# Splitting rows into pieces on GpSimd inside the dense stage, and block numbers read 16 at a time, in a three-layer graph network

## What is computed

```python
def _spmm(row, col, vals, x):
    msg = vals[:, None] * x[col]
    return jax.ops.segment_sum(msg, row, num_segments=N)

def _layer(x_prev, row, col, vals, W_a, b_a, W_b, b_b):
    h = _spmm(row, col, vals, x_prev)
    z = (h + x_prev) @ W_a.T + b_a + h * x_prev @ W_b.T + b_b
    return jnp.where(z >= 0, z, NEG_SLOPE * z)

x1 = _layer(x, row, col, vals, W1_1, b1_1, W1_2, b1_2)
x2 = _layer(x1, row, col, vals, W2_1, b2_1, W2_2, b2_2)
x3 = _layer(x2, row, col, vals, W3_1, b3_1, W3_2, b3_2)
return jnp.concatenate((x, x1, x2, x3), axis=1)
```

## Time and profile before

| | us |
|---|---|
| median of 3 runs | 8891.55 |
| the profiled execution | 8889.35 |
| its span, first to last instruction | 8887.5 |
| expand stages, three together | 2430.5 |
| dense stage, each | 78.7 |
| last row of `xb` written to first matmul of the next layer | 33.7 |

### The profile page before, as it was taken

One profiled execution on the slowest core, in us unless ns is written; L12 is line 12 of the kernel. 1 busy time (PEld: TensorE's weight loads), 2 busy tenths in 40 slices (PEclk: granted clock), 3 DMA queues, 4 the chain that ended last, 5 costly groups with the idle time before them and its releaser, 6 DMA issues.

```text
span 8887.5 us, 265258 instructions
## 1 busy us (share of the span) xinstructions
PE 7889.6 (89%) x82756; PEld 7229.6 (81%) x82757; DVE 7142.9 (80%) x9830; ACT 4541.7 (51%) x14097; POOL 5736.8 (65%) x4886
## 2 busy tenths in 40 slices
PE   5999995799996688899999788899999788899999
PEld 4777775577774588789999788899999688799999
DVE  8999988799997877777777777777777777777777
ACT  0999990799995366621112566611112566611112
POOL 4787874588883244478886344478885444488884
PEclk8999995899997799999999899999999899999999
DMA  2111111211111488788887588888886688888885
GB/s 79 7 7 7 7 7 39 34 7 7 7 7 26 159 295 294 289 286 283 286 286 244 204 296 295 302 277 286 286 286 220 228 295 290 296 283 286 286 286 199
DMA packets 877540, 1680.36 MB, mean 189 GB/s; under 512 B 262122, under 2 KB 313399, under 8 KB 876404
## 3 DMA queue, kind: packets, MB, share of 16 engines
q0 software_dynamic: 364832, 907.43, 34.4%
q1 hardware_dynamic: 499692, 758.75, 24.0%
q10 hardware_dynamic: 12520, 6.40, 0.2%
HBM read 912.31 MB, written 759.79 MB: 188 GB/s over the span
## 4 chain that ended last, share of the span: by engine, by line
PE 45%; ACT 19%; issue 12%; DMA 8%; SPq 7%; DVE 5%; POOL 1%; ACTq 1%; DVEq 0%; POOLq 0%
PE ps L1037 35%; ACT hT L723 17%; DMA messages<-work 7%; SPq L684 6%; PE ps L1028 5%; PE ps L864 1%; DVE hT L1348 1%; SPq L669 1%; DVE hT L1134 1%; PE ps L1065 1%; PE ps L1045 1%; PE ps L1066 1%; PE ps L891 1%; POOL work L575 1%; DVE work L1385 1%
## 5 line engine op out<-in xcount | busy, mean ns | idle before, releaser
L1037 PE MATMUL ps<-work 128*128 128x125 f32 x26880 | 3111.5, 278 | 52.6 <-DVE work L1414 52.6
L1037 PEld LDWEIGHTS ps<-work 128*128 128x128 f32 x26880 | 3066.2, 192 | 97.9 <-DVE work L1414 57.4
L603 POOL DMA_INDIRECT work<-messages,work x1680 | 2567.6, 1528 | 557.7 <-issue 550.0
L1028 PE MATMUL ps<-xb,work 125*128 x10752 | 1992.4, 226 | 450.9 <-DVE work L1385 265.8
L792 ACT ACTIVATE work<-ps,work 128x128 f32<-128x128 f32 x5376 | 1526.9, 371 | 1073.4 <-PE ps L1028 572.0
L1414 DVE TENSOR_TENSOR work<-work,iota_p 128x1000 f32<-128x1000 f32 x1680 | 2005.2, 1194 | 1.0 <-ACT work L810 0.4
L1028 PE MATMUL ps<-hT,work 125*128 x10752 | 1991.7, 224 | 0.4
L1028 PE MATMUL ps<-work 125*128 x10752 | 1976.6, 224 | 0.8
L810 ACT ACTIVATE work<-work 128x8 f32<-128x8 f32 x1680 | 516.2, 307 | 2527.8 <-DMA work<-messages,work 2527.8
L917 PEld LDWEIGHTS ps<-hT 128*128 128x128 f32 x12768 | 1484.1, 196 | 297.1 <-ACT stage L712 227.9
L917 PE MATMUL ps<-hT 128*128 128x96 f32 x12768 | 1520.1, 280 | 186.6 <-ACT stage L712 186.5
(11 more groups left out here) (212 smaller groups left out, 6096.0 us busy)
## 6 DMA issues: line engine op xcount, KB each, us to landing
messages<-work SPq DMA_DIRECT2D x2688, 258.0 KB, 4.0
work<-messages,work POOLq DMA_INDIRECT x1680, 5.9
out_x<-xb SPq DMA_DIRECT2D x150, 125.0 KB
sorted_edges<-stage,run_idx POOLq DMA_INDIRECT x798
work<-slot_cols SPq DMA_DIRECT2D x672, 4.0 KB
work<-lane_places SPq DMA_DIRECT2D x532, 5.2 KB, 2.1
out_x<-xb ACTq DMA_DIRECT2D x4, 1562.5 KB
sorted_edges<-hT SPq DMA_DIRECT2D x4, 908.0 KB
```

The costliest lines, as they stand in the source:

```text
L603: pool.indirect_dma_start(out=ck[:, n, :, :].rearrange("p j e -> p (j e)"), out_offset=None, in_=messages, in_offset=bass.IndirectOffsetOn ...
L1028: last = t.matmul(ps[:, n % PR, j * D:(j + 1) * D], col_hot[:, at:at + P], piece[:, bass.ds(offset, D)], start=k == 0, stop=k == 2)
L1037: last = t.matmul(part[n], ck[:, n, j, 0:D], sel[:, n % SELB, j, :], start=j == 0, stop=j == CHB - 1)
```

## The change

First, the split of the rows for the second and third layer. VectorE now splits only the input rows, once, ahead of the layer loop. In the dense stage of every layer, the last too, GpSimd runs 50 steps: it waits until ScalarE has written the two blocks of the step into `xb` and VectorE has read the columns of `hT` that are to be written over (three sums ahead), makes `rest` for 256 columns (125 x 256), waits for that instruction, and makes `x_low` for them. TensorE waits for the last step (`pieces_cut`) where it waited for VectorE's pieces.

Second, TensorE's block numbers. The table is read as bytes: one load takes 16 bytes into 16 registers and serves 16 groups, so the loop has 56 passes a layer instead of 14 and a quarter of the code, and the shift and mask are gone.

```diff
+                def cut_pieces(i, last):
+                    for k in range(DU):
+                        at = bass.ds(i * (DU * 2 * D) + k * 2 * D, 2 * D)
+                        pool.wait_ge(sum_ready, la * DSTEPS + i * DU + (min(k + 3, DU) if last else k + 3))
+                        pool.wait_ge(xb_ready, la * DSTEPS + i * DU + (k + 2))
+                        taken_up()
+                        g.tensor_tensor(rest[:, at], x_flat[:, at], x_high[:, at], ALU.subtract).then_inc(rest_cut, 1)
+                        pool.wait_ge(rest_cut, la * DSTEPS + i * DU + (k + 1))
+                        taken_up()
+                        g.tensor_tensor(x_low[:, at], rest[:, at], x_mid[:, at], ALU.subtract).then_inc(pieces_cut, 1)
+                with pool.Fori(0, DSTEPS // DU - 1) as i:
+                    cut_pieces(i, False)
+                cut_pieces(DSTEPS // DU - 1, True)
...
-                pe.wait_ge(pieces_ready, la * SPLITS + SPLITS)
+                pe.wait_ge(pieces_ready, SPLITS)
+                pe.wait_ge(pieces_cut, la * DSTEPS + 1)
                 pe.sem_inc(pe_layers, 1)
-                with pe.Fori(0, ABODIES // LB) as i:
-                    _, four = nc.values_load_multi_w_load_instructions(
-                        group_at[0:1, bass.ds(i * (LB * AU // 4), LB * AU // 4)], engines=[mybir.EngineType.PE],
...
-                    for n in range(LB * AU):
-                        offset = ((four[n // 4] >> (n % 4 * 8)) & 255) * D
+                with pe.Fori(0, ABODIES) as i:
+                    _, block_of = nc.values_load_multi_w_load_instructions(
+                        group_at[0:1, bass.ds(i * AU, AU)], engines=[mybir.EngineType.PE],
...
+                    for n in range(AU):
...
-                                                piece[:, bass.ds(offset, D)], start=k == 0, stop=k == 2)
+                                                piece[:, bass.ds(block_of[n] * D, D)], start=k == 0, stop=k == 2)
...
+            dve.wait_ge(x0_got, NB * DMA)
+            W = HTW // SPLITS
+            for c in range(SPLITS):
+                at = slice(c * W, (c + 1) * W)
+                v.tensor_tensor(rest[:, at], x_flat[:, at], x_high[:, at], ALU.subtract).then_inc(rest_ready, 1)
...
             with dve.Fori(0, LAYERS) as la:
...
-                for c in range(SPLITS):
-                    at = slice(c * W, (c + 1) * W)
-                    v.tensor_tensor(rest[:, at], x_flat[:, at], x_high[:, at], ALU.subtract).then_inc(rest_ready, 1)
-                dve.wait_ge(rows_kept, GPP)
-                for c in range(SPLITS):
-                    at = slice(c * W, (c + 1) * W)
-                    dve.wait_ge(rest_ready, la * SPLITS + (c + 1))
-                    v.tensor_tensor(x_low[:, at], rest[:, at], x_mid[:, at], ALU.subtract).then_inc(pieces_ready, 1)
```

More of the change, by code:

```diff
@@ L84 @@
 ABODIES = GROUPS // AU
-LB = 4
 CHB = 8
@@ L263, in graph_layers @@
         base_of = work[:, TBL0 + TB:TBL0 + 2 * TB]
[L264 to L266 removed]
+        group_at = wu[0:1, 4 * (TBL0 + 2 * TB):4 * (TBL0 + 2 * TB) + GROUPS]
+        assert 4 * TBL0 % 16 == 0 and TB % 2 == 0 and AU % 16 == 0 and NB <= 256
         row_at = wi[0:1, TBL0 + 2 * TB + GROUPS:TBL0 + 3 * TB + GROUPS]
@@ L365, in graph_layers @@
         pieces_ready = sem("pieces_ready")
+        rest_cut = sem("rest_cut")
+        pieces_cut = sem("pieces_cut")
         col_hot_ready = sem("col_hot_ready")
@@ L499, in _ @@
             pool.sem_inc(xb_ready, 1)
+            pool.sem_inc(pieces_cut, 1)
             def taken_up():
@@ L557, in _ @@
             with pool.Fori(0, LAYERS) as la:
+                pool.wait_ge(pieces_cut, la * DSTEPS + 1)
                 def put_rows(i, n, first):
@@ L1011, in _ @@
                 pe.wait_ge(xb_ready, la * DSTEPS + 1)
-                pe.wait_ge(pieces_ready, la * SPLITS + SPLITS)
+                pe.wait_ge(pieces_ready, SPLITS)
+                pe.wait_ge(pieces_cut, la * DSTEPS + 1)
                 pe.sem_inc(pe_layers, 1)
-                with pe.Fori(0, ABODIES // LB) as i:
-                    _, four = nc.values_load_multi_w_load_instructions(
-                        group_at[0:1, bass.ds(i * (LB * AU // 4), LB * AU // 4)], engines=[mybir.EngineType.PE],
-                        min_val=0, max_val=(NB - 1) * 0x01010101,
-                        skip_runtime_bounds_check_because="the table holds four numbers of blocks in each word")
-                    for n in range(LB * AU):
-                        offset = ((four[n // 4] >> (n % 4 * 8)) & 255) * D
-                        offset.max_val = (NB - 1) * D
+                with pe.Fori(0, ABODIES) as i:
+                    _, block_of = nc.values_load_multi_w_load_instructions(
+                        group_at[0:1, bass.ds(i * AU, AU)], engines=[mybir.EngineType.PE],
+                        min_val=0, max_val=NB - 1, skip_runtime_bounds_check_because="the table holds numbers of blocks")
+                    for n in range(AU):
                         if n % 2 == 0:
-                            pe.wait_ge(col_hot_ready, la * (GROUPS // 2) + i * (LB * AU // 2) + (n // 2 + 1))
-                        pe.wait_ge(msg_ready[n % 2], la * (GROUPS // 2) + i * (LB * AU // 2) + (n // 2 + 1))
+                            pe.wait_ge(col_hot_ready, la * (GROUPS // 2) + i * (AU // 2) + (n // 2 + 1))
+                        pe.wait_ge(msg_ready[n % 2], la * (GROUPS // 2) + i * (AU // 2) + (n // 2 + 1))
                         for j in range(CH):
@@ L1357, in _ @@
             dve.wait_ge(tabs_done, 1)
+            dve.wait_ge(x0_got, NB * DMA)
[3 more added lines that the diff above has]
+                v.tensor_tensor(rest[:, at], x_flat[:, at], x_high[:, at], ALU.subtract).then_inc(rest_ready, 1)
+            dve.wait_ge(rows_kept, GPP)
+            for c in range(SPLITS):
+                at = slice(c * W, (c + 1) * W)
+                dve.wait_ge(rest_ready, c + 1)
+                v.tensor_tensor(x_low[:, at], rest[:, at], x_mid[:, at], ALU.subtract).then_inc(pieces_ready, 1)
             with dve.Fori(0, LAYERS) as la:
```

5 lines of the change are left out of this document (2 added, 3 removed).

## The result

| | before | after | ratio, 95% interval |
|---|---|---|---|
| median of 4 runs | 8894.65 us (8888.81 to 8904.67) | 9650.85 us (9650.04 to 9655.8) | 1.085 (1.0831 to 1.0869) |
| expand stages, three together | 2430.5 us | 3220 us | |
| gap to the next expand stage, twice | 33.7 us | 17.0 and 17.2 us | |
| last row of `xb` to the end | 4.2 us | 16.7 us | |

The change makes the kernel 8.5% slower: +756 us. The forecast was 8755 us, faster, with a range up to 8970. The stages tell where the time went. These are stretches of the kernel after: the first dense stage, the gap behind it, and the last dense stage with the end of the program (length, then busy time of PE, PEld, VectorE, ScalarE, GpSimd, PEclk, DMA share, GB/s). The earlier trace rows are the same stretches of before.

What follows compares the result with a forecast made beforehand. The prediction took the stores, not TensorE, to pace the expand stages in steady flow, with a stop every pass. From 8889.35 us, -18 (split) and -118 (block numbers) gave 8753, stated as 8755 us for the median; range 8635 to 8970.

Steps and rivals of the forecast that it cites:

- The load: Head of each expand pass: 16 bytes into registers take 1.1 us, bounds 0.5 and 1.8; the pause is 1.4 us.
- The branch: End of each expand pass: the shorter loop body stays at hand, so the branch takes 0.21 us instead of 4186 ns.
- Rival (d): Expand loop: the smaller body is fetched anew too, each pass losing 8.4 us; about 9720 us, chance 0.07.
- The pace: Expand stages: filled buffers cover the pause, stores set the pace; 0.86 us a group for 0.904, -118 us.
- Rival (c): Head of each expand pass: the pauses are not covered, 0.94 us a group; about 8970 us, chance 0.14.
- The split: Dense stage and gaps: GpSimd's step takes 1.8 us, two gaps gain 14.8 us each, the end loses 12; -18 us.

Runs made afterwards that it cites:

- e5: The changed kernel with four block numbers packed in a 32-bit word, 8 words for 32 groups, 28 passes; 8690.44 us, 0.9748 of the kernel before.
- e3: The changed kernel with the block-number table in 32-bit words, one for each group, 16 a load; 8719.92 us, 0.9788 of the kernel before.
- e4: The changed kernel with four block numbers packed in a 32-bit word, 4 words for 16 groups, shift and mask back; 8688.57 us, 0.9749 of before.
- e11: e3 with its load of 16 words made twice a pass; 9275.53 us in a single run, against 8919.68 of the kernel before.
- e6: e4 with one tiny GpSimd product behind the last gather of each layer; 8676.35 us, 0.9733 of the kernel before.
- e13: e6 without the last layer's cuts, and with the last 6 of 50 steps cut by VectorE; 8664.11 us, 0.9719 of the kernel before.
- e14: e13 with a small broadcast of 8 columns right behind GpSimd's last cut; 8649.74 us, 0.9704 of the kernel before.
- e10: The changed kernel with its bytes loaded four at a time, ahead of every fourth group; 8890.03 us in a single run, against 8919.68 of before.

## Why the prediction was wrong

It named the right parts, and the split came out nearly as worked out. It fell on one term of the block numbers, a sentence of the step "The load": "Bytes instead of words should not make it longer. I take 1.1 us, bounds 0.5 and 1.8." It was 6.24 us. All its rows were of loads of 32-bit words; no load of a byte stood in them, and instead of leaving that bound open upward it was closed by what seemed plausible. The rest followed: a pause of 1.4 us is covered, one of 6.2 us is not.

Step by step:

- *The branch*: forecast 0.21 us, measured 213 ns. Instruction packets in the whole run fell from 453 to 84, and the queue of the earlier trace rows has none between 5210 and 6270 us, in the second expand stage. The Trainium skill ("Advanced Engine Details and Errata", section "ISA Cache") has "Only 2 cache lines" of 256 instructions; a pass of e5, with 32 groups, has 956 instructions in its trace, and its branch too takes 213 ns. So for TensorE the measurement decides against that line. The prediction's own argument against it, the 272 instructions of line 1032, was too weak: two lines of 256 would hold them, unless one is taken by what is fetched ahead. Rival (d), a body fetched anew, did not happen.
- *The load*: 1.1 us forecast, 6.24 measured. This step failed. With words in the same loop (e3) it is 2.10 us, above my upper bound too: in the flow of the stage a load of 16 takes 1.6 to 1.9 times its quickest (6.24 for 3.78, 2.10 for 1.10). I had put the 1763 ns of before down to the instruction packets, but e3 has as few of them as the kernel after, 84 in the whole run, and is slower. Why a load is slower in the flow stays open.
- *The pace*: 0.86 us forecast for a covered pause; e4 has 0.839, e3 0.853. The mechanism held, and the stores' own pace is a little better than the 0.853 read out of the late stretches. The DMA share is 0.87 there, as forecast. With the pause of the forecast the kernel would have come out near e4 or e3: 8689 and 8720 us on a chip where the kernel before takes 8913, under the 8755 I said, within its range.
- *Rival (c)*, the pause not covered, is the mechanism that decided. Its point of decision, a slack of 2.4 us in a pass, fits: 2.1 us (e3) is covered, 4.4 us (e11) is not, and nothing between was tried. Its clock term holds as well: 6.2 us of standing, then 4.9 us at 0.50. Its price, 8970 us, was worked out with 1.4 us, and it puts the pause on top of the stores' pace. With 6.2 us that way of counting gives 16 x 0.853 + 6.2 = 19.8 us a pass. What the trace shows is another sum, the pause on top of TensorE's own need, 16 x 0.70 + 6.2 = 17.4 us, plus about 2 us of clock (47 matmuls in 4.9 us for 2.7): 19.4, and it measured 19.1. That rival (d)'s 9720 us lies near the result is chance.
- *The split*: a cut forecast at 0.62 us, measured 613 and 636 ns (medians of lines 617 and 620). A step forecast at 1.8 us, measured 1.36 to 1.52: the lower bound. The cut waits for the one before it 0.25 us (37.6 us in 150 times) and not 0.34, and the 0.2 us ahead of the first and for the lock are hardly there. VectorE's busy time in the dense stage rises from 54.06 to 56.28 us, and the stage by 0.6. What I missed is the pause at the change of kind, 6.9 us before the first cut and 5.5 before the broadcast; a row for it, 5.7 us, was in the trace of the kernel before. I had 2.8 us from the last cut to the first matmul, and it is 5202.5 - 5194.6 = 7.9. The slow step that did not come and the pauses that were not seen nearly cancel, and that is luck: gaps of 17.0 instead of 19, a tail of +12.5 instead of +12, -21 us in sum for -18.
- *The range*: it ended at 8970 because the price of the load had no room upward. The cuts on GpSimd had no row of their shape either, but two rows bounded them, and the measured step lay at the lower bound. The load of bytes had no row of its width, and its upper bound was a load of words.

## What to carry to other kernels

Read TensorE's register values as 32-bit words, several small numbers in each, and shift and mask them out: e4 does just that in the short loop and is 2.5% faster than the kernel before where bytes are 8.5% slower. Shortening a loop whose branch is dear was right; set the number of values that it reads at its head against the slack of the engine behind it (here 2.2 us), because a stop beyond that costs its length and clock on top. When an engine gets a new kind of work between two old kinds, look for what lies ahead of its first instruction, and if it is GpSimd's pause between broadcasts and products, take it with a tiny instruction of that kind some 6 to 10 us early.

## What the runs showed of the hardware

- A TENSOR_LOAD into TensorE's registers costs 0.07 to 0.08 us for each 32-bit word at its quickest (1102 ns for 16, 590 for 8, 329 for 4) and 0.24 us for each byte or 16-bit half (3784 and 3786 ns for 16, 983 for 4). In the flow of the expand stage it is 0.13 to 0.15 for a word and 0.39 for a byte or half (0.31 where four bytes are loaded at a time). Why narrow values are dear no run shows.
- Loop bodies of 452 (after), 480 (e4) and 956 (e5) instructions of TensorE come back in 213 ns; the one of 1908 (before) takes 4.2 us. The edge lies between the last two and was not looked for.
- GpSimd's first broadcast behind products begins 5.5 to 6.0 us after a MODIFY_POOL_CONFIG (before, after, e6, e13, e14), its first product behind broadcasts 6.9 to 7.0 us after one (after) and 8.2 to 10.2 us where it is taken up in the gather stage (e6, e13, e14). Behind gathers alone it is 0.1 us (before). The Trainium skill ("GPSIMD Engine Reference", section "2.1 Instruction dispatch") gives approximately 6 us for the first call to a freshly loaded kernel, and the trace agrees for the broadcasts: 5.6 us in e13, 5.7 in e14. The pause starts only when the instruction is taken up, after its semaphore wait (e13).
- Four stops of 1.23 us in 14.6 us leave TensorE's granted clock at 1.00 (e10); one stop of 6.2 us in 19.1 brings it to 0.50 for the 4.9 us behind it.
